# The operand of the selection's iterations placed in a PSUM bank instead of SBUF

## The chip, the core and the metric

The kernel runs on one core of one Trainium2 chip. The metric is device time in microseconds (us). Engines are called by the profile's names: PE is TensorE, PEld its weight loads, DVE is VectorE, ACT is ScalarE, POOL is GpSimd and SP is SyncE.

## The reference, cut to what matters

The input is 16 sequences of 256 tokens with 128 features. A first part normalises, modulates and runs causal attention with one head on each sequence and adds the result to the input. A second part normalises and modulates again and adds two attentions with eight heads: a light one in windows of 128 tokens, and a heavy one whose 128 queries are picked by a routing score and whose keys are all 256 tokens. The routing is what the change touches:

```python
def coor_descent(s, k):
    logk = jnp.log(jnp.asarray(k, s.dtype))
    def body(_, ab):
        a, b = ab
        a = EPS * (logk - jax.nn.logsumexp((s + b) / EPS, axis=-1, keepdims=True))
        b = -jax.nn.relu(s + a)
        return (a, b)
    a, b = jax.lax.fori_loop(0, N_ITERS, body, (jnp.zeros_like(s[..., :1]), -s))
    return jnp.exp((s + a + b) / EPS)
...
scores = coor_descent(s, k)                       # s: 16 x 256, for queries and for keys; 50 iterations
sel_scores, sel_idx = jax.lax.top_k(scores, num_tokens)
```

## The kernel before, in words

Each engine has its own instruction list. All lists are written by one function, `run_slots`, which walks over slots t and calls, in a fixed order within the slot, the stages that fall due: phase A (the first attention, one sequence every two to three slots), phase L (the light attention, a sequence every four slots), phase H (the heavy attention, a sequence every four slots, after the selection) and T (work tied to a slot number). An engine executes its list in that order; semaphores tie the engines together.

The selection handles 32 rows at once (16 sequences, for queries and keys), on 32 partitions with 256 elements each. In slot SCORES_AT + 1 PE transposes the scores into `ps[1][0:32, 0:256]`. `cd_start` (L1166) copies them to `s_rows` and makes the shifted scores `cd_t`; ACT writes their exponentials to `cd_e` (L532). Then `cd_iteration` (L1176) runs 49 times on DVE: one scalar_tensor_tensor (L1183) takes the minimum of `cd_e` and a per-row scalar `u`, multiplies it by the constant tile `inv_k`, writes `cd_min`, and sums each row into the next `u`, which the next iteration waits for. The 49 iterations come in three segments (17, 16 and 16); between segments `cd_rebase` (L1186) makes a new `cd_t` from a logarithm by ACT (L536) and ACT writes `cd_e` again, so L532 runs three times. In DVE's list, up to two iterations at a time stand at three places of a slot (`select_1`, `select_2`, `select_3`), between the instructions of the light attention: the maxima `nmx` (L1137), the reciprocals `rinv` (L1143) and the copies of projections and values out of PSUM (L1114, L1126, L1131). Sixteen rounds of a search for the eight largest follow (`top_round`, L1198), then the chosen rows are packed and transposed through `ps[1]`.

What the light attention makes of the instructions named: ACT's exponentials (L571) wait for `nmx`; POOL's `normalise` (L400) waits for `rinv` and multiplies the 128x512 tile `pr` in place; PE's `p_transpose` (L795) waits for POOL; `scores` (L781) waits for the copies of queries and keys (L1114 on DVE); `values` is L811 and `project_v` L640 to L642. POOL also adds the light result to `X` (L405).

Bank 1 of PSUM serves the first attention until its last output is read (PE waits for that in `selection`, L729), then the scores, and later the packed selection and phase H's row transposes. The light attention uses banks 0, 2, 3, 4, 6 and 7.

Of the kernel before, what the change touches and what calls it, by code (L numbers as in the profile page):

```python
# [8 lines left out]
ACT = mybir.ActivationFunctionType  # L9
# [6 lines left out]
B, N, D = 16, 256, 128  # L16
# [45 lines left out]
def adaln_routed_attention(nc, x, w_attn, b_attn, gamma_l, wq_l, wkv_l, wo_l, q_tok, kv_tok,  # L62
                           gamma_h, wq_h, wkv_h, wo_h, c, wmod, out):
    with ExitStack() as ctx:
        def sb(name, shape, dt=F32):
            return ctx.enter_context(nc.sbuf_tensor(name, shape, dt))

        def sem(name):
            return ctx.enter_context(nc.semaphore(name))

        ps = [ctx.enter_context(nc.psum_tensor(f"bank{i}", [P, 512], F32)) for i in range(8)]
# [37 lines left out]
        R = 2 * B  # L109
        na_first = sb("na_first", [R, 1])  # L110
        inv_k = sb("inv_k", [R, N])
# [51 lines left out]
        sb = lambda name, shape, dt=F32: early.enter_context(nc.sbuf_tensor(name, shape, dt))  # L163
# [19 lines left out]
        sb = late  # L183
# [6 lines left out]
        smax = sb("smax", [R, 1])  # L190
        cd_c = sb("cd_c", [R, 1])
        cd_t = sb("cd_t", [R, N])
        cd_e = sb("cd_e", [R, N])
        cd_min = sb("cd_min", [R, N])
        cd_u = [sb(f"cd_u{i}", [R, 1]) for i in two]
        cd_ln = sb("cd_ln", [R, 1])
# [30 lines left out]
        r = {n: sem("r_" + n) for n in (  # L227
            "Sd", "Sp", "rows", "smax", "c", "t", "e", "u", "ln", "na", "sc", "top", "at", "left", "w1", "w", "t1", "selp",
            "selT")}
# [216 lines left out]
        def _(act):  # L446
# [81 lines left out]
            def cd_act(t):  # L528
                if t in (SCORES_AT + 3, LN_AT[0] + 1, LN_AT[1] + 1):
                    s = (SCORES_AT + 3, LN_AT[0] + 1, LN_AT[1] + 1).index(t)  # L530
                    act.wait_ge(r["t"], s + 1)
                    act.activation(cd_e[:, :], cd_t[:, :], ACT.Exp).then_inc(r["e"], 1)  # L532
                if t in LN_AT:
                    n = SEGMENTS[LN_AT.index(t) + 1]
                    act.wait_ge(r["u"], n)
                    act.activation(cd_ln[:, :], cd_u[(n - 1) % 2][:, :], ACT.Ln).then_inc(r["ln"], 1)  # L536
                if t == LN_AT[2] + 1:
                    act.wait_ge(r["t"], 4)
                    act.activation(score[:, :], cd_t[:, :], ACT.Exp).then_inc(r["sc"], 1)
# [78 lines left out]
            def pt_evac_h(b, u):  # L618
                g = 4 * b + u
                act.wait_ge(hv["PTp"], g + 1)  # L620
                if g == 0:
# [3 lines left out]

            run_slots([("A", 6, pt_evac_a), ("H", 8, pt_evac_h, 3), ("H", 3, k_evac_h), ("L", 7, pt_evac_act, 2),
                       ("A", 5, exps_a), ("T", 0, cd_act), ("H", 6, exps_h, 3), ("L", 6, pt_evac_act, 1),
                       ("A", 2, h_evac), ("L", 5, exps, 2), ("L", 3, k_evac_l), ("H", 5, exps_h, 1), ("L", 2, q_evac_l),
                       ("L", 4, exps, 0), ("H", 6, pt_evac_h, 0), ("A", 13, xt_hi), ("H", 5, exps_h, 2),
# [295 lines left out]
        def _(dve):  # L925
# [250 lines left out]
            def cd_iteration(n):  # L1176
                if n in SEGMENTS:
                    dve.wait_ge(r["e"], SEGMENTS.index(n) + 1)
                    u = u_first
                else:  # L1180
                    dve.wait_ge(r["u"], n)
                    u = cd_u[(n - 1) % 2]
                dve.scalar_tensor_tensor(cd_min[:, :], cd_e[:, :], u[:, :], inv_k[:, :], ALU.min, ALU.mult,  # L1183
                                         accum_out=cd_u[n % 2][:, :]).then_inc(r["u"], 1)

            def cd_rebase(s):  # L1186
# [42 lines left out]
            def iterations(t, part):  # L1229
                if t in ITERATIONS_AT:  # L1230
                    first, end = ITERATIONS_AT[t]
                    for n in range(first + 2 * part, min(end, first + 2 * part + 2)):
                        cd_iteration(n)
# [105 lines left out]
```

## Time and profile before

| | |
|---|---|
| median of three runs | 505.95 us (503.81 to 508.93) |
| the profiled execution, its own time | 505.71 us |
| its span, first to last instruction | 503.9 us |
| busy share of the span | PE 89%, PEld 78%, DVE 70%, ACT 69%, POOL 52% |
| L1183, main instruction of the iterations | 46 with 25.1 us, 3 with 2.2 us |
| mean granted PE clock | 0.986 of full |

The profiled execution's time holds 1.8 us beside its span. A share is an average over stages that differ: the iterations lie between about 209 and 260 us of the span.

### The profile page before, as it was taken

The page shows a single profiled execution, that of the slowest core. Times are in us where ns is not written, and L with a number is a line of the kernel's source. Part 1 is how long each engine was busy: PE and PEld are TensorE (multiplying, and loading weights), DVE is VectorE, ACT ScalarE, POOL GpSimd, SP SyncE. Part 2 cuts the span into 40 slices and gives each one's busy share as a digit, 9 for nine tenths or more (in the row PEclk, how much of TensorE's full clock was granted, in tenths as well). Part 3 has the DMA queues.
Part 4 walks back from the last instruction along what each step waited for, and adds up shares of the span by engine and source line. Part 5 has one row for each costly group of instructions (what it writes and reads, how often), then busy time and mean ns, then how long its engine had stood idle before and what let it go on. Part 6 is the DMA issues. An engine that isn't in the chain of part 4 may idle for free.

```text
span 503.9 us, 11927 instructions
## 1 busy us (share of the span) xinstructions
PE 447.9 (89%) x4021; PEld 390.6 (78%) x4021; DVE 351.1 (70%) x1130; ACT 345.9 (69%) x1260; POOL 264.3 (52%) x297
## 2 busy tenths in 40 slices
PE   2676888999899989988987989999999999999994
PEld 1464777888898977877876878788988889888883
DVE  6767788788778997889889984446455655546551
ACT  2168888778798868757767657766766777666761
POOL 7316566375476666241333324554565566655555
PEclk9999999999999999989999889999999999999998
DMA  8850000000001010000000000100011000100002
GB/s 227 274 232 23 13 11 12 12 23 23 12 23 32 3 33 22 22 12 2 12 12 11 12 2 18 33 17 7 6 17 20 12 10 12 17 17 12 7 7 21
DMA packets 18107, 16.26 MB, mean 32 GB/s; under 512 B 1952, under 2 KB 16816, under 8 KB 17792
## 3 DMA queue, kind: packets, MB, share of 16 engines
q1 hardware_dynamic: 14048, 11.70, 7.2%
q0 software_dynamic: 3248, 3.41, 4.0%
q8 instruction: 32, 0.52, 0.4%
q10 hardware_dynamic: 752, 0.40, 0.3%
q14 instruction: 27, 0.22, 0.1%
HBM read 10.23 MB, written 5.28 MB: 31 GB/s over the span
## 4 chain that ended last, share of the span: by engine, by line
PE 48%; DVE 13%; issue 4%; POOL 4%; ACT 3%; POOLq 0%; ACTq 0%; DVEq 0%
PE bank L873 6%; PE bank L884 5%; PE bank L899 5%; PE bank L640 4%; PE bank L781 4%; PE bank L642 4%; PE bank L641 4%; PE bank L840 3%; DVE cd_min L1183 3%; PE bank L811 3%; PE bank L911 2%; ACT pr L571 2%; PE bank L795 2%; DVE nmx L1137 2%; PE bank L822 2%
## 5 line engine op out<-in xcount | busy, mean ns | idle before, releaser
L400 POOL TENSOR_TENSOR pr<-pr,rinv 128x512 f32<-128x512 f32 x64 | 67.3, 1051 | 103.1 <-DVE rinv L1143 102.7
L412 POOL TENSOR_TENSOR pr<-pr,rinv 128x512 f32<-128x512 f32 x64 | 72.7, 1156 | 63.6 <-DVE rinv L1288 63.6
L571 ACT ACTIVATE pr<-bank,nmx 128x128 f32<-128x128 f32 x256 | 90.3, 377 | 22.4 <-DVE nmx L1137 22.4
L614 ACT ACTIVATE pr<-bank,nmx 128x256 f32<-128x256 f32 x128 | 59.3, 485 | 19.3 <-DVE nmx L1282 19.3
L1282 DVE TENSOR_REDUCE nmx<-bank 128x2 f32<-128x512 f32 x64 | 41.9, 681 | 35.0 <-PE bank L873 35.0
L624 ACT ACTIVATE pt<-bank 128x512 f32<-128x512 f32 x64 | 38.2, 597 | 27.7 <-PE bank L884 27.7
L571 ACT ACTIVATION_READ_ACCUMULATOR pr<-bank,nmx 128x1 f32 x256 | 55.7, 218 | 0.0
L795 PE MATMUL bank<-ident,pr 128*128 128x128 f32 x256 | 39.8, 279 | 13.3 <-POOL pr L400 11.6
L1137 DVE TENSOR_REDUCE nmx<-bank 128x4 f32<-128x512 f32 x64 | 42.3, 673 | 7.4 <-PE bank L781 7.2
L795 PEld LDWEIGHTS bank<-ident,pr 128*128 128x128 f32 x256 | 29.7, 142 | 19.6 <-POOL pr L400 14.2
L884 PE MATMUL bank<-ident,pr 128*128 128x128 f32 x256 | 38.9, 274 | 2.3 <-ACT pt L624 2.3
L781 PE MATMUL bank<-KT,QT 64*128 64x128 f32 x512 | 36.9, 300 | 0.8 <-DVE KT L1114 0.5
L781 PEld LDWEIGHTS bank<-KT,QT 64*128 64x128 f32 x512 | 34.0, 209 | 4.0 <-issue 3.8
L583 ACT ACTIVATE pt<-bank 128x512 f32<-128x512 f32 x35 | 21.2, 605 | 21.3 <-PE bank L795 21.3
L884 PEld LDWEIGHTS bank<-ident,pr 128*128 128x128 f32 x256 | 29.2, 140 | 5.9 <-POOL pr L412 2.0
L873 PE MATMUL bank<-KT,QT 64*128 64x256 f32 x256 | 32.0, 389 | 0.0
L899 PEld LDWEIGHTS bank<-pt,V 128*64 128x64 f32 x512 | 27.6, 137 | 5.1 <-issue 5.1
L811 PE MATMUL bank<-pt,V 128*64 128x128 f32 x512 | 31.6, 276 | 0.0
L899 PE MATMUL bank<-pt,V 128*64 128x128 f32 x512 | 31.5, 276 | 0.0
L822 PE MATMUL bank<-wo_l_sb,oT 128*128 128x128 f32 x256 | 31.3, 275 | 0.0
L1268 DVE COPY KT<-bank 128x512 f32<-128x512 f32 x16 | 11.1, 692 | 28.7 <-PE bank L642 28.7
L822 PEld LDWEIGHTS bank<-wo_l_sb,oT 128*128 128x128 f32 x256 | 29.8, 192 | 0.0
(222 smaller groups left out, 1319.9 us busy)
## 6 DMA issues: line engine op xcount, KB each, us to landing
mod_bc<-mod_rows_scratch SPq DMA_DIRECT2D x1, 3072.0 KB, 11.4
X<-in_L_attn_x SPq DMA_DIRECT2D x4, 512.0 KB, 9.3
xh_scratch<-xhs SPq DMA_DIRECT2D x16, 128.0 KB, 1.9
out<-X SPq DMA_DIRECT2D x16, 128.0 KB, 1.8
mod_bc<-mod_rows_scratch SPq DMA_DIRECT2D x1, 1024.0 KB, 4.3
wkv_raw<-in_L_ffn_wkv_light SPq DMA_DIRECT2D x1, 512.0 KB, 11.3
wmod_sb<-in_L_wmod ACTq DMA_DIRECT2D x1, 384.0 KB, 5.4
wq_raw<-in_L_ffn_wq_heavy POOLq DMA_DIRECT2D x1, 256.0 KB, 6.7
```

The lines of the kernel that those rows point to most:

```text
L400: pool.tensor_tensor(q, q, rinv[u][:, :, None].broadcast_to([P, 4, P]), ALU.mult)\
L412: pool.tensor_tensor(q, q, rinv[u][:, 0:2, None].broadcast_to([P, 2, N]), ALU.mult)\
L571: act.activation(pr[u][:, i * P:(i + 1) * P], ps[bank][:, i * P:(i + 1) * P], ACT.Exp, bias=nmx[u][:, i:i + 1], accum_out=sums[u][:, i:i + ...
L614: act.activation(pr[u][:, i * N:(i + 1) * N], ps[bank][:, i * N:(i + 1) * N], ACT.Exp, bias=nmx[u][:, i:i + 1], accum_out=sums[u][:, i:i + ...
L781: mm = pe.matmul(ps[SCORE_BANKS[w][i]][:, c * P:(c + 1) * P], QT[b % 2][rows, c, t], KT[b % 2][rows, c, t], start=True, stop=True)
L795: mm = pe.transpose(ps[4][:, i * P:(i + 1) * P], pr[u][:, i * P:(i + 1) * P], ident[:, :])
L811: mm = pe.matmul(ps[VALUE_BANKS[w]][i * DH:(i + 1) * DH, q * P:(q + 1) * P], V[b % 2][:, w, h * DH:(h + 1) * DH], pt[2 * w + i][:, q * P:( ...
L822: mm = pe.matmul(ps[6][:, w * D:(w + 1) * D], oT[w][:, q, :], wo_l_sb[:, q, :], start=(q == 0), stop=(q == 3))
L873: mm = pe.matmul(ps[SCORE_BANKS[n][i]][:, m * N:(m + 1) * N], QT[b % 2][rows, c, 0:NQ], KT[b % 2][rows, c, :], start=True, stop=True)
L884: mm = pe.transpose(ps[4][:, i * P:(i + 1) * P], pr[u][:, i * P:(i + 1) * P], ident[:, :])
L899: mm = pe.matmul(ps[6][i * DH:(i + 1) * DH, c * NQ:(c + 1) * NQ], V[b % 2][:, w, h * DH:(h + 1) * DH], pt[2 * n + i][:, (2 * m + w) * P:(2 ...
L1137: dve.tensor_reduce(nmx[u][:, :], ps[SCORE_BANKS[u // 2][u % 2]][:, :].rearrange("p (h t) -> p h t", h=4), AX.X, ALU.max, negate=True).the ...
```

## The change: where the exponentials lie

ACT's exponentials of the three segments go to the first 256 columns of bank 1 on 32 partitions, where the scores had been, and the iterations read them there. The SBUF tile `cd_e` is gone. No instruction is added, removed or moved, and every wait stays.

```diff
-        cd_e = sb("cd_e", [R, N])
...
-                    act.activation(cd_e[:, :], cd_t[:, :], ACT.Exp).then_inc(r["e"], 1)
+                    act.activation(ps[1][0:R, 0:N], cd_t[:, :], ACT.Exp).then_inc(r["e"], 1)
...
-                dve.scalar_tensor_tensor(cd_min[:, :], cd_e[:, :], u[:, :], inv_k[:, :], ALU.min, ALU.mult,
+                dve.scalar_tensor_tensor(cd_min[:, :], ps[1][0:R, 0:N], u[:, :], inv_k[:, :], ALU.min, ALU.mult,
                                          accum_out=cd_u[n % 2][:, :]).then_inc(r["u"], 1)
```

## Rows read from the trace of the kernel before

**Rows 1.** The page, chain of work that ended last: shares of the span by engine.

```profile
PE 48%; DVE 13%; issue 4%; POOL 4%; ACT 3%; POOLq 0%; ACTq 0%; DVEq 0%
```

**Rows 2.** Busy time by stage: stretch, length; PE, PEld, DVE, ACT, POOL; clock, DMA.

```profile
246.00:260.00 14.00, 12.77 (x125) 10.89 (x126) 13.30 (x43) 9.54 (x39) 4.19 (x4) 1.00 0.04 11
```

**Rows 3.** View of line L1183: durations in ns as min/median/max.

```profile
L1183 DVE SCALAR_TENSOR_TENSOR cd_min<-cd_e,cd_u,inv_k x46: 443/473/1135, 210.7 to 259.7; 32x256 f32<-32x256 f32 x46
...
L1183 DVE SCALAR_TENSOR_TENSOR cd_min<-cd_e,u_first,inv_k x3: 463/465/1300, 209.4 to 246.3; 32x256 f32<-32x256 f32 x3
```

**Rows 4.** Timeline of DVE, long iterations: start us, duration us, instruction, [idle before].

```profile
209.39 1.30 DVE L1183 SCALAR_TENSOR_TENSOR cd_min<-cd_e,u_first,inv_k 32x256 f32<-32x256 f32 x1 [0.47 <-ACT cd_e L532]
...
215.35 1.13 DVE L1183 SCALAR_TENSOR_TENSOR cd_min<-cd_e,cd_u,inv_k 32x256 f32<-32x256 f32 x1
...
230.26 1.14 DVE L1183 SCALAR_TENSOR_TENSOR cd_min<-cd_e,cd_u,inv_k 32x256 f32<-32x256 f32 x1
...
240.12 0.89 DVE L1183 SCALAR_TENSOR_TENSOR cd_min<-cd_e,cd_u,inv_k 32x256 f32<-32x256 f32 x1
...
241.05 0.83 DVE L1183 SCALAR_TENSOR_TENSOR cd_min<-cd_e,cd_u,inv_k 32x256 f32<-32x256 f32 x1
...
255.99 1.13 DVE L1183 SCALAR_TENSOR_TENSOR cd_min<-cd_e,cd_u,inv_k 32x256 f32<-32x256 f32 x1
```

**Rows 5.** Timeline of POOL around 215 us.

```profile
214.97 1.24 POOL L400 TENSOR_TENSOR pr<-pr,rinv 128x512 f32<-128x512 f32 x1 [4.56 <-DVE rinv L1143]
```

**Rows 6.** Timelines of DVE and POOL at 103 us, and views of L1062 and L1097.

```profile
103.74 0.61 DVE L1062 SCALAR_TENSOR_TENSOR ao<-bank,rinva,mod_bc 128x128 f32<-128x128 f32 x2 [0.69 <-PE bank L713]
...
103.48 1.04 POOL L400 TENSOR_TENSOR pr<-pr,rinv 128x512 f32<-128x512 f32 x1
...
L1062 DVE SCALAR_TENSOR_TENSOR ao<-bank,rinva,mod_bc x32: 335/344/353, 32.9 to 182.6; 128x128 f32<-128x128 f32 x32
...
L1097 DVE CUSTOM_DVE_ANT_0 rprod<-h,tok_bc x64: 260/286/1164, 39.8 to 197.3; 128x128 f32<-128x128 f32 x64
```

**Rows 7.** Views of L1002 and L1000: the same operation on SBUF and on PSUM.

```profile
L1002 DVE SCALAR_TENSOR_TENSOR K_w_lo<-wkv_raw,gam_col,K_w_hi x1: 751/751/751, 23.8 to 23.8; 128x512 fp32r<-128x512 f32 x1
L1002 DVE SCALAR_TENSOR_TENSOR KH_w_lo<-bank,gam_col,KH_w_hi x1: 751/751/751, 26.6 to 26.6; 128x512 fp32r<-128x512 f32 x1
...
L1000 DVE TENSOR_SCALAR K_w_hi<-wkv_raw,gam_col x1: 481/481/481, 23.3 to 23.3; 128x512 fp32r<-128x512 f32 x1
L1000 DVE TENSOR_SCALAR KH_w_hi<-bank,gam_col x1: 740/740/740, 25.8 to 25.8; 128x512 fp32r<-128x512 f32 x1
```

**Rows 8.** View of L532, and timeline of ACT at 204 us.

```profile
L532 ACT ACTIVATE cd_e<-cd_t x3: 400/401/415, 209.0 to 244.8; 32x256 f32<-32x256 f32 x3
...
204.04 0.39 ACT L525 ACTIVATE XT_hi<-bank 128x256 fp32r<-128x256 f32 x1
```

**Rows 9.** Timelines of DVE and PE around 232 and 246 us.

```profile
232.16 2.06 PE L781 MATMUL bank<-KT,QT 64*128 64x128 f32 x32 [0.33 <-DVE KT L1114]
...
245.36 0.69 DVE L1114 COPY KT<-bank 128x512 f32<-128x512 f32 x1 [0.66 <-PE bank L642]
...
246.46 2.06 PE L781 MATMUL bank<-KT,QT 64*128 64x128 f32 x32
```

**Rows 10.** Timeline of PE after long gaps, and the granted clock of one stretch.

```profile
216.27 1.00 PE L795 MATMUL bank<-ident,pr 128*128 128x128 f32 x4 [2.95 <-POOL pr L400]
217.25 3.28 PE L781 MATMUL bank<-KT,QT 64*128 64x128 f32 x32
...
261.44 0.66 PE L795 MATMUL bank<-ident,pr 128*128 128x128 f32 x4 [1.15 <-POOL pr L400]
...
293.83 0.65 PE L795 MATMUL bank<-ident,pr 128*128 128x128 f32 x4 [2.21 <-POOL pr L400]
294.62 3.54 PE L781 MATMUL bank<-KT,QT 64*128 64x128 f32 x32
...
218.00:220.00 2.00, 2.00 (x24) 2.00 (x22) 1.92 (x9) 0.00 (x0) 0.00 (x0) 0.54 0.05 12
```

## Prediction

> **What bounds the kernel now.** I first read the chain of work that ended last: PE carries 48% of the span and DVE 13% [rows 1], so DVE matters only where the chain passes through it. The chain in order of time showed where: between 209 and 300 us, in the selection. Busy time by stage confirms it: from 246 to 260 us DVE works 13.30 of 14.00 us [rows 2], while PE there waits for what DVE hands on. In that stretch an instruction removed from DVE, or shortened, can move the end; the change touches just these, the 49 iterations.
>
> The view of their line shows two kinds: the median iteration takes 473 ns, the longest 1135, and of the three that open a segment the median is 465 and the longest 1300 [rows 3]. The timeline names eight long ones, six of them in [rows 4]; the other two, at 253.67 and 254.60 us, repeat the pair at 240.12 and 241.05. Their excess over the median: 0.83, 0.66, 0.67, 0.42, 0.36, again 0.42 and 0.35, and 0.66, together 4.37 us.
>
> What they share is POOL. At 215.35 us DVE starts an iteration while POOL's `normalise` runs from 214.97 to 216.21; the iteration ends with it [rows 4, 5]. POOL's own 1.24 us is 0.20 above the 1.04 that the same instruction takes elsewhere [rows 5, 6], so each holds up the other. Is it any DVE instruction, or only one with two tensors in SBUF? L1062 has the form that the changed iteration will have (one tensor in PSUM, a scalar and one tensor in SBUF): two of them lie wholly inside a `normalise`, from 103.74 to 104.35 us within 103.48 to 104.52, and take 0.61 us together; over all 32 the longest is 353 ns against a median of 344 [rows 6]. L1097, with both tensors in SBUF, goes from 286 to 1164 ns [rows 6]. So one tensor in PSUM is enough to end the quarrel.
>
> **The change, part by part.** *The contention goes.* Every long iteration falls back to about 470 ns: 4.37 us less on DVE. What of it moves the end, from place to place:
> - At 209.39: 0.83 us. The copy of queries, the rest of the iterations and the reciprocal that POOL awaits at 214.97 stand behind it in DVE's list, and PE has stood idle 2.95 us for POOL when it resumes at 216.27 [rows 5, 10]. POOL's own 0.20 us lies on the same path. Sum 1.03.
> - At 215.35: 0.66 us, costed at nothing. PE meanwhile works on what POOL handed over, and the maxima that follow on DVE need PE's scores. Without this cover (if PE ran faster there) it would count; that is a rival below.
> - At 230.26: 0.67 us. The copy of keys stands right behind it and PE waits for that copy before its scores at 232.16 [rows 9]; DVE's list then runs on. All 0.67 counted.
> - At 240.12 and 241.05: 0.78 us. Here PE is next in line: the copy of keys at 245.36 waits 0.66 for PE [rows 9], and PE's work before it hangs on a reciprocal ahead of these two iterations. That copy ends at 246.05 and the scores start at 246.46, so 0.41 is slack that can go and 0.37 is lost. Counted 0.41.
> - At 253.67, 254.60 and 255.99: 0.42 + 0.35 + 0.66 = 1.43 us. DVE is full here [rows 2], and PE waits 1.15 us at 261.44 for a POOL result that waits for DVE [rows 10]. All counted.
>
> The sum is 1.03 + 0.67 + 0.41 + 1.43 = 3.54 us. After it come the 16 rounds of the search, which fill DVE, and the heavy attention, both unchanged and started by what is now earlier, so I let the gain run through to the end.
>
> *The iteration reads PSUM.* No iteration does so before, so the price is bounded by neighbours. The nearest is L1002, also a scalar_tensor_tensor with a scalar per partition: 751 ns with its first tensor in SBUF and 751 in PSUM [rows 7]. The far end is L1000, where the same swap costs 740 against 481 ns for 512 elements [rows 7], half of it, 0.13 us, for 256; but there it is the SBUF form that is uncommonly fast (481 ns for 512 elements, with a single tensor), and the iteration, 473 ns for 256, has no such speed to lose. A gain per iteration is not excluded, but L1062 speaks against one: 344 ns for 128 elements [rows 6] plus 128 more at L1002's rate ((751 - 344) / 384 = 1.06 ns each, an estimate) is 480. I take 0, with +0.13 and -0.03 (the 443 of the shortest, [rows 3]) as ends.
>
> The Trainium skill, Perfetto Trace Analysis, section Optimizing Scalar/DVE Operations, gives DVE about 60 ns of access overhead per instruction on SBUF and about 125 on PSUM. That speaks against this change: an estimate by that page is 49 x 65 ns = 3.2 us more on DVE, and by it 0.8 x 3.2 = 2.5 of the gain would be eaten, which leaves 504.7 us. The rows of L1002 disagree with it for this kind of instruction, and I follow the rows.
>
> *ACT writes PSUM.* Three instructions of 0.40 us [rows 8]. None in the trace writes there; one of 256 elements that reads PSUM takes 0.39, so I take 0 and bound it at 0.1 us either way for each. DVE waits for the first alone (0.47 us, [rows 4]).
>
> No wait, DMA or instruction is added. Bank 1 is idle for PE between the scores' transposes and the packed selection, so no queue gets a new neighbour.
>
> The profiled execution took 505.71 us, 0.24 below the median of the runs shown. 505.71 - 3.54 = 502.2 us; against the median it would be 502.4. I say **502.3**.
>
> **The rivals.**
> - *PE's clock no longer falls.* After idling 2.95 us PE runs its scores in 3.28 us instead of 2.06, with a granted clock of 0.54 (the lower level, 1.2 GHz) [rows 9, 10]. The gap shrinks to 2.95 - 1.03 = 1.92 us. After a gap of 2.21 the clock had also fallen (3.54 us); after 1.15 it had not (0.66 for the transposes) [rows 10]. 1.92 lies nearer the former. If the clock holds, DVE's 0.66 at 215.35 counts too, and the gain rises by 0.5 to 1.1 us: 501.2 to 501.7.
> - *PSUM is dearer, and it ends slower than before.* One mechanism: each iteration waits for the previous sum, so a longer read of bank 1 adds to every step. About 0.8 of the iterations lie where DVE sets the pace (3.54 of 4.37), some 39. The gain is gone from 3.54 / 39 = 0.09 us per iteration; at the far end, 0.13, it is 39 x 0.13 - 3.54 = 1.5 us slower: 507.2. At half of it, 504.7. For it: the 740 against 481. Against it: the 751 against 751, the same operation.
> - *The contention stays.* `inv_k` and the scalar still come from SBUF; if that alone makes DVE wait for POOL, nothing changes: 505.7. L1062 [rows 6] has just these operands and speaks against it.
> - *Covered more than I count.* The long iterations only hide waits for PE or ACT that then show: half the sum, 1.8 us, 503.9.
>
> **How the numbers follow.** Forecast (502.3, from 501.7 to 503) 0.50; clock held 0.17; covered more 0.13; PSUM dearer 0.13, of which 0.06 ends slower than before; contention stays 0.07. The runs before spread by about 0.5% to either side. The range from 500.6 to 505.0 takes in the first three cases, the milder half of the fourth, and some of that spread; what lies outside is the dear PSUM, the unchanged kernel and a gain larger than I can add up. What a measurement can tell from no change is about 1%, 5 us. Faster by more than that needs all 4.37 us, POOL's share and the clock: 0.16. Slower by more than 5 us needs a price above the far end: 0.04. Within 1%: 0.80.
>
> **What would show it.** Right: the longest iteration of L1183 near 0.48 us and none at 0.8 or more; the short ones still at 0.47; POOL's `normalise` at 1.04 between 209 and 260 us; the last iteration some 3.5 us earlier. Wrong: iterations at 0.53 us or more throughout (PSUM is dearer), long ones that remain beside POOL (contention stays), or new waits of DVE for PE or ACT in place of the long iterations (covered). PE's scores near 217 us at 2.06 instead of 3.28 us would show the clock rival. What I can't place is the rebase (L1190), whose length depends on where POOL happens to run.

## The result: faster by 0.9%, and the profile after

Sixteen runs of the changed kernel have a median of 501.79 us (500.47 to 504.75), sixteen of the kernel before one of 506.52 (503.81 to 510.89): a ratio of 0.9906, with a 95% interval from 0.9885 to 0.9927. The forecast was 502.3 us in a range from 500.6 to 505.0. The profiled execution of the changed kernel took 501.88 us (span 500.1), 3.83 less than that of before. One line was taken out, so the line numbers of after are lower by one.

The view of the iterations' line answers [rows 3]; below it stands the line by which ACT writes the exponentials, which answers [rows 8]. Durations are ns as min/median/max.

```profile
L1182 DVE SCALAR_TENSOR_TENSOR cd_min<-bank,cd_u,inv_k x46: 442/470/473, 209.5 to 255.8; 32x256 f32<-32x256 f32 x46
...
L1182 DVE SCALAR_TENSOR_TENSOR cd_min<-bank,u_first,inv_k x3: 461/461/470, 209.0 to 244.1; 32x256 f32<-32x256 f32 x3
...
L531 ACT ACTIVATE bank<-cd_t x3: 359/360/377, 208.6 to 242.3; 32x256 f32<-32x256 f32 x3
```

The longest of the 49 iterations takes 473 ns; before it was 1300. They have not become shorter or longer otherwise: median 470 against 473. They still run beside POOL. In the timelines of DVE and POOL, at the places of [rows 4, 5], two iterations lie in whole or nearly so inside a `normalise`, and neither engine is held up:

```profile
208.97 0.47 DVE L1182 SCALAR_TENSOR_TENSOR cd_min<-bank,u_first,inv_k 32x256 f32<-32x256 f32 x1 [0.43 <-ACT bank L531]
...
214.09 0.47 DVE L1182 SCALAR_TENSOR_TENSOR cd_min<-bank,cd_u,inv_k 32x256 f32<-32x256 f32 x1
...
208.99 1.04 POOL L399 TENSOR_TENSOR pr<-pr,rinv 128x512 f32<-128x512 f32 x1
213.71 1.04 POOL L399 TENSOR_TENSOR pr<-pr,rinv 128x512 f32<-128x512 f32 x1 [3.68 <-DVE rinv L1142]
```

The page's shares of the chain answer [rows 1], and the busy time of the stretch that corresponds to [rows 2] (2 us earlier) shows DVE as full as before, 13.38 of 14.00 us, with 48 instructions instead of 43:

```profile
PE 49%; DVE 11%; POOL 4%; issue 4%; ACT 3%; POOLq 0%; ACTq 0%; DVEq 0%
```

```profile
244.00:258.00 14.00, 12.71 (x127) 11.03 (x126) 13.38 (x48) 10.22 (x41) 4.81 (x5) 1.00 0.04 11
```

**Where the time went.** PE's scores (L781 before, L780 after) come once per sequence and serve as marks. The timeline of PE after, which answers [rows 9, 10]:

```profile
200.34 2.06 PE L780 MATMUL bank<-KT,QT 64*128 64x128 f32 x32
...
214.81 0.66 PE L794 MATMUL bank<-ident,pr 128*128 128x128 f32 x4 [1.88 <-POOL pr L399]
215.39 3.10 PE L780 MATMUL bank<-KT,QT 64*128 64x128 f32 x32
218.42 2.52 PE L810 MATMUL bank<-pt,V 128*64 128x128 f32 x32
...
230.14 2.06 PE L780 MATMUL bank<-KT,QT 64*128 64x128 f32 x32
...
244.01 2.06 PE L780 MATMUL bank<-KT,QT 64*128 64x128 f32 x32
...
257.51 0.66 PE L794 MATMUL bank<-ident,pr 128*128 128x128 f32 x4 [1.10 <-POOL pr L399]
258.10 2.06 PE L780 MATMUL bank<-KT,QT 64*128 64x128 f32 x32
```

Before, the scores started at 200.72, 217.25, 232.16, 246.46 and 262.02 us. Counted from the first mark:

| up to the scores near | before | after | saved | forecast, summed up |
|---|---|---|---|---|
| 217 us | 16.53 | 15.05 | 1.48 | 1.03 |
| 232 us | 31.44 | 29.80 | 1.64 | 1.70 |
| 246 us | 45.74 | 43.67 | 2.07 | 2.11 |
| 262 us | 61.30 | 57.76 | 3.54 | 3.54 |

From there to the end of the light attention the distance stays (3.47 us at the last scores, 309.15 us before and 305.30 after). The first mark itself lies 0.38 us earlier after; that is ahead of everything the change touches and not part of it: 3.54 + 0.38 = 3.92, against 3.8 between the spans.

### The profile page after: what moved, and what is told of

It reads as the page before. It is cut to its first block, busy times and chain, and to the rows that moved or that the text cites. A ratio compares the mean times of both kernels' runs of the same rounds, so it can differ in the third digit from the quotient of the medians.

```text
span 500.1 us, 11927 instructions
## 1 busy us (share of the span) xinstructions
PE 447.7 (90%) x4021; PEld 390.7 (78%) x4021; DVE 346.6 (69%) x1130; ACT 346.5 (69%) x1260; POOL 263.8 (53%) x297
## 4 chain that ended last, share of the span: by engine, by line
PE 49%; DVE 11%; POOL 4%; issue 4%; ACT 3%; POOLq 0%; ACTq 0%; DVEq 0%
PE bank L872 6%; PE bank L883 5%; PE bank L898 5%; PE bank L780 4%; PE bank L639 4%; PE bank L641 4%; PE bank L640 4%; PE bank L810 4%; PE bank L839 3%; PE bank L910 3%; DVE cd_min L1182 2%; ACT pr L570 2%; PE bank L794 2%; POOL pr L399 2%; PE bank L821 2%
## 5 line engine op out<-in xcount | busy, mean ns | idle before, releaser
L780 PE MATMUL bank<-KT,QT 64*128 64x128 f32 x512 | 36.7, 299 | 0.6 <-DVE KT L1113 0.2
L780 PEld LDWEIGHTS bank<-KT,QT 64*128 64x128 f32 x512 | 33.7, 207 | 3.5 <-issue 3.3
L898 PEld LDWEIGHTS bank<-pt,V 128*64 128x64 f32 x512 | 27.6, 137 | 5.1 <-issue 5.1
L810 PEld LDWEIGHTS bank<-pt,V 128*64 128x64 f32 x512 | 28.5, 140 | 2.5 <-issue 1.3
```

What stands on the lines that cost most here:

```text
L780: mm = pe.matmul(ps[SCORE_BANKS[w][i]][:, c * P:(c + 1) * P], QT[b % 2][rows, c, t], KT[b % 2][rows, c, t], start=True, stop=True)
L810: mm = pe.matmul(ps[VALUE_BANKS[w]][i * DH:(i + 1) * DH, q * P:(q + 1) * P], V[b % 2][:, w, h * DH:(h + 1) * DH], pt[2 * w + i][:, q * P:( ...
L898: mm = pe.matmul(ps[6][i * DH:(i + 1) * DH, c * NQ:(c + 1) * NQ], V[b % 2][:, w, h * DH:(h + 1) * DH], pt[2 * n + i][:, (2 * m + w) * P:(2 ...
```

## The experiments

Open were three things: whether the collision, and not the address, ACT's write or the first operand, explains the iterations; whether the path is as the forecast drew it; and why the medians differ by 4.7 us where the two profiled executions differ by 3.8.

**The tile kept (`tile_kept`).** The change, with the tile of SBUF allocated but unused:

```diff
+        cd_e = sb("cd_e", [R, N])
```

> The change with the SBUF tile of the exponentials still allocated, unused, so that no other tile changes its address. Theory (iterations with two SBUF tensors and POOL hold each other up; worth 3.5 us between 209 and 262 us): 3.5 us faster than before, ratio 0.993, longest iteration 0.48 us, the scores after the iterations (before at 262.02 us) 3.5 us earlier against the start of the iterations. Rival (the 4.7 us between the medians hold something else, such as shifted tile addresses, which act on the rest of the kernel): the iterations the same, but a ratio nearer 0.996 than that of the change (0.9906).

Measured: 501.52 us against 506.86 for the kernel before on the same chip, ratio 0.9898 (0.9863 to 0.9933). The last mark lies 57.80 us after the first (57.76 without the tile). Addresses play no part; but the gap between the medians did not shrink to 3.5 us either, so the first theory is not the whole account.

**The other tensor in PSUM (`inv_k_psum`).** The exponentials back in SBUF, the constant tile copied to bank 1:

```diff
+                dve.tensor_copy(ps[1][0:R, N:2 * N], inv_k[:, :]).then_inc(r["ik"], 1)
...
+                    dve.wait_ge(r["ik"], 1)
...
-                dve.scalar_tensor_tensor(cd_min[:, :], cd_e[:, :], u[:, :], inv_k[:, :], ALU.min, ALU.mult,
+                dve.scalar_tensor_tensor(cd_min[:, :], cd_e[:, :], u[:, :], ps[1][0:R, N:2 * N], ALU.min, ALU.mult,
```

> The kernel before with the other tensor, inv_k, copied once into the upper half of bank 1 and read there; the exponentials stay in SBUF. Theory (two SBUF tensors are what collides, no matter which leaves): iterations 0.44 to 0.48 us, none long, 3.5 us less 0.0 to 0.4 for the added copy, ratio 0.993 to 0.994. Rival (only the first tensor's place counts, or what helps is that ACT writes PSUM): long iterations of 0.8 to 1.3 us remain, ratio 1.000.

Measured: 501.06 us, ratio 0.9894 (0.9864 to 0.9923). The view of its iterations and PE's timeline:

```profile
L1185 DVE SCALAR_TENSOR_TENSOR cd_min<-cd_e,cd_u,bank x46: 438/469/470, 209.6 to 254.6; 32x256 f32<-32x256 f32 x46
```

```profile
200.37 2.06 PE L781 MATMUL bank<-KT,QT 64*128 64x128 f32 x32
...
214.86 0.66 PE L795 MATMUL bank<-ident,pr 128*128 128x128 f32 x4 [1.68 <-POOL pr L400]
215.44 2.06 PE L781 MATMUL bank<-KT,QT 64*128 64x128 f32 x32
...
256.95 2.06 PE L781 MATMUL bank<-KT,QT 64*128 64x128 f32 x32
```

No iteration is over 470 ns: it is enough that one of the two tensors leaves SBUF, whichever, and ACT's write to PSUM isn't needed. It came out better than expected (0.993 to 0.994): here the gap ahead of the scores was 1.68 us, and the scores ran in 2.06 us instead of 3.10. The last mark lies 56.58 us after the first, where the change has 57.76 and the kernel before 61.30. So this trace prices the clock rival of the prediction: 1.18 us more than the change saves, where 0.5 to 1.1 was forecast. The copy costs nothing: the first iteration starts 3.33 us after the copy of the scores, as before, because it waits for ACT's exponentials.

**POOL writes only (`pool_write_only`).** The kernel before, with the normalisation of the light attention replaced:

```diff
-                pool.tensor_tensor(q, q, rinv[u][:, :, None].broadcast_to([P, 4, P]), ALU.mult)\
+                pool.memset(q, 0.0)\
```

> The kernel before, with POOL's normalise of the light attention (L400) replaced by a memset of the same tile: it waits and signals as before, writes 128x512 and reads nothing; the light attention's weights are left out of the result. Theory (what collides is DVE's second read with POOL's reads): no iteration beside L400 is long, those beside L405, which reads two tensors, are still up to 0.9 us. Rival (any POOL access to SBUF, writes too, holds up an instruction with two SBUF tensors): iterations beside the memset are as long as its remainder, up to the memset's duration.

Measured: one run, 492.94 us, not to be compared, as work is left out. DVE's and POOL's timelines:

```profile
206.78 0.47 DVE L1183 SCALAR_TENSOR_TENSOR cd_min<-cd_e,cd_u,inv_k 32x256 f32<-32x256 f32 x1
...
230.42 0.83 DVE L1183 SCALAR_TENSOR_TENSOR cd_min<-cd_e,cd_u,inv_k 32x256 f32<-32x256 f32 x1
...
206.89 0.52 POOL L400 MEMSET pr<- 128x512 f32 x1 [4.78 <-DVE rinv L1143]
...
229.96 1.02 POOL L405 TENSOR_TENSOR X<-X,tmp 128x256 f32<-128x256 f32 x1
...
258.18 0.41 DVE L1214 TENSOR_TENSOR sel<-score,w1m 32x256 f32<-32x256 f32 x1
...
258.03 0.59 POOL L400 MEMSET pr<- 128x512 f32 x1 [0.67 <-DVE rinv L1143]
```

The iteration at 206.78 runs beside a memset and takes its 0.47 us; the one at 230.42 runs beside L405, which reads, and takes 0.83, while L405 itself takes 1.02 instead of 0.73. Only two iterations are long, both beside L405. By themselves the iterations are a weak test: those that begin inside a memset have at most 0.19 us of it left, too little to tell a hold from none. Other instructions with two tensors in SBUF settle it. The sum of the key weights (L1214) begins 0.15 us into a memset and takes 0.41 us; in the kernel before it begins 0.13 us into a `normalise` and takes 1.18:

```profile
270.27 1.18 DVE L1214 TENSOR_TENSOR sel<-score,w1m 32x256 f32<-32x256 f32 x1
...
270.14 1.04 POOL L400 TENSOR_TENSOR pr<-pr,rinv 128x512 f32<-128x512 f32 x1 [0.16 <-DVE rinv L1143]
```

And fourteen products of the routing (L1097) begin inside a memset, with up to 0.52 us of it left, and all take 0.28 or 0.29 us; in the kernel before, the five that begin inside a `normalise` with about 1 us left take 1.11 to 1.16. With two tensors in SBUF, DVE collides with POOL's reads and not with a write alone. The Trainium skill, SBUF — State Buffer, section Who interferes with whom, says so: a DVE instruction with two SBUF inputs contends with a GpSimd instruction that reads SBUF and not with one that only writes. For these instructions the two traces agree.

**One segment at a time (`seg_first`, `seg_last`).** Exponentials in PSUM for segment 0 alone, or for segment 2 alone (`(2,)` in the first line), with the iterations reading the same place; the edit is to the kernel before:

```diff
+        cd_es = [ps[1][0:R, 0:N] if i in (0,) else cd_e[:, :] for i in range(3)]
...
-                    act.activation(cd_e[:, :], cd_t[:, :], ACT.Exp).then_inc(r["e"], 1)
+                    act.activation(cd_es[s], cd_t[:, :], ACT.Exp).then_inc(r["e"], 1)
...
-                dve.scalar_tensor_tensor(cd_min[:, :], cd_e[:, :], u[:, :], inv_k[:, :], ALU.min, ALU.mult,
+                e = cd_es[max(i for i in range(3) if SEGMENTS[i] <= n)]
+                dve.scalar_tensor_tensor(cd_min[:, :], e, u[:, :], inv_k[:, :], ALU.min, ALU.mult,
```

> Only the first segment's exponentials in PSUM, the other two in SBUF. Theory (two long iterations go, 0.83 and 0.66 us, and POOL's 0.20; only 1.0 us of it was on the path, the clock may add 0.5): the scores that started at 232.16 us in before start 1.0 to 1.5 us earlier against those at 200.72; five or six long iterations remain beside POOL's L400 and L405 in the later segments. Rival (all of the excess counts wherever it lies): 1.7 us.

> Only the last segment's exponentials in PSUM. Theory (three long iterations go, 0.42, 0.35 and 0.66 us, all on the path): the scores that started at 262.02 us in before start 1.4 us earlier, counted from those at 246.46 us, and nothing changes ahead of them; 15.56 us between the two becomes 14.1. Rival (PE or ACT wait in place of DVE): 15.0 or more.

One run of each; their times are not compared, only the marks. PE's timelines of the first and of the second:

```profile
200.94 2.06 PE L782 MATMUL bank<-KT,QT 64*128 64x128 f32 x32
...
231.28 2.06 PE L782 MATMUL bank<-KT,QT 64*128 64x128 f32 x32 [0.32 <-DVE KT L1115]
...
260.58 0.68 PE L796 MATMUL bank<-ident,pr 128*128 128x128 f32 x4 [1.14 <-POOL pr L401]
261.19 3.61 PE L782 MATMUL bank<-KT,QT 64*128 64x128 f32 x32
```

```profile
246.88 2.06 PE L782 MATMUL bank<-KT,QT 64*128 64x128 f32 x32
...
260.99 2.06 PE L782 MATMUL bank<-KT,QT 64*128 64x128 f32 x32
```

With the first segment alone the mark near 232 comes at 30.34 instead of 31.44 us: 1.10 saved, inside the range expected, not the 1.69 of the whole excess; six long iterations remain later. The clock has a part in this 1.10, which the section on the prediction takes up. With the last alone the distance of its two marks is 14.11 instead of 15.56 us: all of the 1.43. One thing was not foreseen: in `seg_first` the scores at 261.19 took 3.61 us, where the profiled execution of before had 2.06.

**PE kept busy in its gaps.** That row pointed to PE's clock as the missing piece. Matmuls that nobody reads, on a free bank, go ahead of the transposes that end a gap:

```diff
+            def keep_busy(b):
+                n = {8: 9, 12: 9, 13: 7}.get(b, 0)
+                if n:
+                    pe.wait_ge(a["xlo"], B)
+                for i in range(n):
+                    pe.matmul(ps[5][:, :], V_w[0][:, 0:P], V_w[0][:, :], start=True, stop=True)
...
-            run_slots([("H", 12, out_heavy), ("L", 2, project_q_l), ("L", 9, values), ("L", 8, p_transpose, 3),
+            run_slots([("H", 12, out_heavy), ("L", 2, project_q_l), ("L", 9, values), ("L", 8, keep_busy), ("L", 8, p_transpose, 3),
```

This is `before_pe_busy`; `pe_busy` is the change with `{8: 6, 12: 9, 13: 7}`.

> The kernel before, with 9, 9 and 7 matmuls without a reader ahead of the transposes that follow PE's three long gaps. Open: the medians differ by 4.7 us and the profiled executions by only 3.8, of which 3.5 us between the first and the last iteration; the runs of before show mean granted clocks from 0.975 to 0.992, those of the change 0.985 to 0.988. Theory (part of the gain between the medians is PE's clock, which the shorter gap in the changed kernel spares): with the gaps filled, before gains 2 to 4 us (ratio 0.993 to 0.996), its runs spread less, and the change is worth 3.5 us over it, not 4.7. Rival (the rest is chance): before gains as much as the change does from the same filling.

> The change, with 6, 9 and 7 such matmuls at the same three places. Theory: scores at 2.06 us in all three places, 3.5 us faster than the kernel before with its gaps filled, ratio to before 0.985 to 0.988. Rival (the clock is a cause of its own and what it spares is independent of the change): 4.7 us faster than that.

Measured on one chip: 503.74 us for before with its gaps filled (ratio to before 0.994, 0.9912 to 0.9969) and 499.27 for the change (0.984, 0.9812 to 0.9868). The first expectation failed in its main point: the distance is 4.5 us, not 3.5. PE's timeline of `before_pe_busy` shows why the test was incomplete: at a fourth gap, which was not filled, the clock fell (granted 0.58 of full speed from 260 to 262 us and 0.56 from 262 to 264, so mostly the lower of its two levels, 1.2 GHz).

```profile
200.13 2.06 PE L781 MATMUL bank<-KT,QT 64*128 64x128 f32 x32
...
260.25 1.07 PE L795 MATMUL bank<-ident,pr 128*128 128x128 f32 x4 [1.15 <-POOL pr L400]
261.25 3.23 PE L781 MATMUL bank<-KT,QT 64*128 64x128 f32 x32
...
307.33 2.06 PE L781 MATMUL bank<-KT,QT 64*128 64x128 f32 x32
```

So the same edit with `11: 4` added on both sides (`before_pe_busy4`, `pe_busy4`):

> The kernel before with its three long gaps of PE filled (9, 9 and 7 matmuls), and 4 more matmuls in a fourth gap, ahead of the transposes that started at 261.44 us. Open: with three gaps filled, the change was still worth 4.5 us, not 3.5. Seen: in that run of before the scores after the fourth gap took 3.23 us at 261.25, in the profiled run of before 2.06 at 262.02; before has two gaps there (1.03 and 1.15 us), the change one (1.10). Theory (in before the clock falls there in part of the executions, and the change removes that too): the scores take 2.06 us there, mean clock 0.997 or more, about 1 us faster than with three gaps filled: ratio to before 0.991 to 0.993, and the change with all four filled is 3.5 to 4 us ahead of it. Rival (the fourth gap's clock costs nothing at the end): ratio 0.994 as before, the distance stays at 4.5 to 4.8 us.

> The change with the same four gaps filled (6, 4, 9 and 7 matmuls). Theory: little against the version with three (the clock rarely falls there in the changed kernel): ratio to before 0.983 to 0.985; from the first scores (201 us) to those near 303 us about 101.5 us, against 105.0 to 105.5 us in the kernel before with the same filling. Rival: 4.5 us or more between the two.

Measured on one chip: 503.34 us (0.9916, 0.9886 to 0.9945) and 499.44 us (0.9843, 0.9803 to 0.9884). PE's timelines, of the former and the latter:

```profile
201.16 2.06 PE L781 MATMUL bank<-KT,QT 64*128 64x128 f32 x32
...
261.85 2.06 PE L781 MATMUL bank<-KT,QT 64*128 64x128 f32 x32
...
306.87 2.06 PE L781 MATMUL bank<-KT,QT 64*128 64x128 f32 x32
```

```profile
200.88 2.06 PE L780 MATMUL bank<-KT,QT 64*128 64x128 f32 x32
...
302.65 2.06 PE L780 MATMUL bank<-KT,QT 64*128 64x128 f32 x32
```

With all scores at full speed the marks lie 105.71 us apart before and 101.77 after: 3.94 us, and 3.90 between the medians. In these two traces this is the change without the clock, and the two ways of measuring agree. With the fourth gap left open, the marks of before lay 107.20 us apart (`before_pe_busy`): the fall of the clock at this one place costs 1.49 us, and beside `pe_busy` (101.78) the change would be worth 5.42.

So an execution of before that loses its clock there is that much worse than the profiled one, and the rest of the 4.7, some 0.8 us, is put down to a part of the executions that do. This size is an estimate: the interval of the ratio puts the gain anywhere from 3.7 to 5.8 us. The clocks of the runs point the same way: of the 39 runs of before beside these experiments, 21 have a mean granted clock of 0.982 or less and a median of 508.0 us, 18 have 0.985 or more and 505.9. The sixteen of the change all have 0.985 to 0.988. Before had two gaps ahead of the scores near 262 us (1.03 us behind a copy by DVE, 1.15 behind POOL), and two near relatives lost the clock there; the change leaves one, of 1.10. That these 21 runs fell at just this gap is not shown. A mean clock does not tell the place: `seg_last` has 0.983 with its scores at 260.99 in 2.06 us. Nor did filling four gaps hold the clock in every execution: 0.997 or more was expected of `before_pe_busy4`, and three of its nine runs reach it, the others have 0.994 or 0.995.

**Further along the same road (`scores_psum`, `scores_psum_pe_busy`).** The exponentials go to columns 256 to 511, the scores stay in bank 1 and are read there, and the intermediate of the key weights takes their place at the end; the second version adds the three fillings of `pe_busy`.

```diff
-        s_rows = sb("s_rows", [R, N])
+        s_rows = ps[1][0:R, 0:N]
...
-        w1m = sb("w1m", [R, N])
+        w1m = ps[1][0:R, 0:N]
...
-                dve.tensor_copy(s_rows[:, :], ps[1][0:R, 0:N]).then_inc(r["rows"], 1)
-                dve.wait_ge(r["rows"], 1)
```

> A further step: the exponentials go to the upper half of bank 1, the scores stay in the lower half and are read there (no copy of them to SBUF), and the intermediate of the key weights is put there too, so that its sum has one tensor in SBUF. Theory (every DVE operation that needs POOL's access to SBUF can be freed so): the rebase that took 1.14 us falls to about 0.42 us, the sum of the key weights from 1.18 to about 0.42, each on the path: 1.4 us more than the change, 5.0 us in all, ratio 0.990. Rival (a PSUM source makes the rebases dearer, 0.41 instead of 0.34, and what is saved is covered by waits for PE): no gain over the change, ratio 0.993.

> The version before this, and PE given 6, 9 and 7 matmuls of 128x512 whose result nobody reads, ahead of the transposes that follow its three long gaps (1.9, 2.7 and 2.2 us in the changed kernel's trace). Theory (the granted clock falls after such gaps, and the scores then take 3.1 to 3.6 us instead of 2.06): the scores take 2.06 us at all three places, and of 1.0 + 1.5 + 1.3 us some 1.0 to 2.5 reach the end, because DVE's list is nearly full there; ratio 0.986 to 0.988. Rival (DVE's list sets the pace, PE's slow scores are hidden by it): scores 2.06 us but no gain, ratio as without them, 0.990. Other rival: the clock falls all the same.

Measured: 500.83 us, ratio 0.9881 (0.985 to 0.9912), and 498.03 us, ratio 0.9827 (0.9794 to 0.986). In the first, the rebase took 0.47 us beside a `normalise` (before 1.14) and the sum of the key weights 0.41 (before 1.18), but the marks from 200 to 305 us came closer by only 1.0 us than in `tile_kept` (103.98 against 104.99), and its median's lead of 0.7 us lies inside the intervals: no gain over the change is shown in time. The clock blurs the marks here, since PE's first long gap was 2.11 us and its transposes already ran in 1.12. With the three gaps filled on both sides the marks are 100.90 us apart, against 101.78 in `pe_busy`: 0.9 of the 1.4 us expected. The second version has the lowest median of all: 1.7% ahead of before, with its scores at 2.06 us in all three places (three gaps filled), as the first theory had it, and its ratio is 0.003 better than the range expected.

## Why the prediction was right, step by step

- *The contention goes*: right, in cause and size. All eight long iterations are at 0.47 us, POOL's 1.24 us at 215 is 1.04 again, and the experiments with different edits agree on the cause. The prediction read that a long iteration ends with POOL's instruction; it ends 0.27 to 0.28 us after it, in all eight cases. And it is the order that decides who is held up. All eight began while POOL's instruction was running. POOL's 1.24 us at 214.97 comes from the iteration before, which was running when POOL began and kept its own 0.47:

```profile
214.84 0.47 DVE L1183 SCALAR_TENSOR_TENSOR cd_min<-cd_e,cd_u,inv_k 32x256 f32<-32x256 f32 x1
```

- *The path*: right to 0.1 us at three of four marks, in part by luck. At the first mark 1.48 us were saved instead of 1.03, because the 0.66 us at 215.35, costed at nothing, was on the path. The copy of keys stands right behind this iteration in DVE's list, and the scores at 217.25 need it. In the profile of before, PE's slow transposes (1.00 us) ended at about the same time and hid the wait. With four gaps filled the transposes take 0.66 us, and PE waits 0.32 us for that copy (first block, `before_pe_busy4`, DVE and PE); counted from the first mark its scores start at 16.54 us, and those of the changed kernel with the same filling at 15.06 (second block, `pe_busy4`): 1.48 again, with the clock held.

```profile
216.88 0.67 DVE L1121 COPY KT<-bank 128x512 f32<-128x512 f32 x1
...
217.70 2.06 PE L781 MATMUL bank<-KT,QT 64*128 64x128 f32 x32 [0.32 <-DVE KT L1121]
```

```profile
215.94 2.06 PE L780 MATMUL bank<-KT,QT 64*128 64x128 f32 x32
```

In the profiled run of the change this 0.45 was given back before the next mark, because its scores and the values behind them took 3.10 and 2.52 us, those of before 3.28 and 1.97:

```profile
220.45 1.97 PE L811 MATMUL bank<-pt,V 128*64 128x128 f32 x32
```

DVE then shows it as waits for PE: the copies `oT` and `V` wait 0.31 and 0.80 us, where there was no wait and 0.62 before. So two things that the sum left out cancelled. `seg_first` had the same: 1.47 us saved at the first mark, 1.10 at the second. Where the clock holds on both sides, the four marks save 1.48, 2.08, 2.49 and 3.95 us; without the 0.67 at 230.26 the first segment is worth 1.41 there. Of the pair near 240 us, what was called lost shows as a longer wait of the copy of keys, 0.96 against 0.66 [rows 9]; ACT takes its part too, since the reciprocal ahead of that copy waits 1.35 us for it, where it waited 0.87 before:

```profile
220.99 0.69 DVE L1130 COPY oT<-bank 128x512 f32<-128x512 f32 x1 [0.31 <-PE bank L810]
...
222.57 0.69 DVE L1125 COPY V<-bank 128x512 f32<-128x512 f32 x1 [0.80 <-PE bank L641]
...
243.18 0.69 DVE L1113 COPY KT<-bank 128x512 f32<-128x512 f32 x1 [0.96 <-PE bank L641]
```

- *The iteration reads PSUM*: 0 was right (470 against 473 ns). L1002 was the neighbour to go by; L1000, which set the far end, was not. It fits its own form: the rebase, a tensor_scalar, took 0.34 us alone from SBUF and 0.47 from PSUM in `scores_psum`, just that 0.13. By the Trainium skill's Perfetto Trace Analysis, section Optimizing Scalar/DVE Operations, each iteration should have paid some 65 ns more, an estimate from its two figures; the measurement decides against it for this form. Where the prediction speaks of 0.8 of the iterations, 3.54 / 4.37 is a share of the excess and not of the iterations, and the 3.54 holds POOL's 0.20.
- *ACT writes PSUM*: 0.36 us instead of 0.40, inside the bound.
- *The clock*: in the profiled execution it fell all the same after a gap of 1.88 us, but later: the transposes still ran in 0.66 us, the scores in 3.10 and the values behind them in 2.52 instead of 1.97. (So the 0.66 us of the transposes after the gap of 1.15, which the prediction took for a sign that the clock had held, is none: the transposes at 293.83 took 0.65, and the scores behind them 3.54 [rows 10]. The scores at 262.02, at 2.06, are the sign.) The rival was wrong for this place in the traces of the change; `inv_k_psum`, where the clock held, shows that its price was near. What the forecast missed is another: the fourth gap, where near relatives of the kernel before lose their clock and the profiled execution did not. The sum was made against an execution that happened to hold it, and so the forecast of 502.3 us came out 0.5 us high and the gain, 3.5 us, 1.2 below the medians' 4.7: 0.4 from the path with the clock held (3.94 against 3.54), which is the 0.45 at 215.35, and 0.8, by the estimate above, from the clock.

## What to carry to other kernels

If an instruction's duration has a narrow median and a few values two to three times as long, lay its timeline beside the other engines' before looking at the instruction: here the long ones all ran beside POOL reading SBUF, and moving either of two operands to a free PSUM bank took the whole excess away at no price per instruction of this form (a single-tensor one paid 0.13 us). Sum the excess along the path, place by place, not in total: of 4.37 us on DVE and 0.20 on POOL, 3.54 reached the last mark, and 3.95 with PE's clock held. And a single profiled execution can hide a state that others of the same kernel have: compare the granted clock of all runs before a gain is put down to one cause.

## What the runs showed of the hardware that was not expected

- PE's clock can fall after gaps of only 1.03 and 1.15 us in close succession: the scores behind them took 2.06 us in the profiled run of before, 3.61 and 3.23 in two near relatives with the same gaps. Such a fall cost 1.49 us at the last scores. Filling four gaps with matmuls that nobody reads gave the kernel before 0.8% (ratio 0.9916).
- The rebase, a tensor_scalar with a single tensor in SBUF, is held up by POOL too: 1.14 us beside a `normalise` in before and after alike, 0.34 alone; with its source in PSUM it takes 0.47 beside one. Beside the memset of `pool_write_only`, which did not disturb the iterations, it took 0.60.
